# Two attention layers on one core: two heads side by side on row and column tiles, instead of one head over two blocks of keys

## The reference

```python
# layer 0, for each head h (16 heads, 64 columns each)
q, k, v = xn @ Wq[h], xn @ Wk[h], xn @ Wv[h]
attn = softmax(q @ k.T * scale)                 # 2048 x 2048
s += (attn @ v) @ WO[rows of head h]
# layer 1: q and k are rotated (rope), and a distance bias of the head is added
attn = softmax(q @ k.T * scale - p[h] * log1p(a[h] * abs(i - j)))
s += (attn @ v) @ out_w.T[rows of head h]
```

## Time and profile before

| | |
|---|---|
| median of 3 runs | 3421.73 us (3419.06 to 3424.5) |
| the profiled execution's own time | 3421.26 us |
| its span | 3419.4 us |
| TensorE (PE) busy | 3133.3 us (92%) |
| VectorE (DVE) busy | 2356.3 us (69%) |
| ScalarE (ACT) busy | 1427.8 us (42%) |
| GpSimd (POOL) busy | 2394.8 us (70%) |
| DMA, mean over the span | 43 GB/s |

### The profile page before, as it was taken

The page is one execution under the profiler, slowest core; times in us unless marked ns, Lnnn a source line. Parts: engine busy times, 40 slices in busy tenths (PEclk is TensorE's granted clock), DMA queues, the critical chain, the costliest instruction groups (busy, mean ns, idle before and its releaser), DMA issues. The chain is left out here.

```text
span 3419.4 us, 47107 instructions
## 1 busy us (share of the span) xinstructions
PE 3133.3 (92%) x18389; PEld 1247.1 (36%) x18389; DVE 2356.3 (69%) x3610; ACT 1427.8 (42%) x1609; POOL 2394.8 (70%) x1080
## 2 busy tenths in 40 slices
PE   5949999999999999948888985999999999999997
PEld 3414444444444444333333431333333333333333
DVE  6545555555555555351211696999999999999996
ACT  3325555555555555510000222555554555545544
POOL 0019999999999999900000383888888888888887
PEclk9969999999999999958888997999999999999998
DMA  3341111112111111010000133111111111112200
GB/s 80 126 123 26 25 26 26 26 26 49 26 26 26 26 26 25 1 51 0 0 0 0 49 148 97 49 49 49 49 49 49 49 49 49 49 54 60 60 23 13
DMA packets 53617, 148.69 MB, mean 43 GB/s; under 512 B 17155, under 2 KB 24076, under 8 KB 51220
## 3 DMA queue, kind: packets, MB, share of 16 engines
q1 hardware_dynamic: 53396, 145.67, 15.5%
HBM read 110.78 MB, written 34.87 MB: 43 GB/s over the span
## 5 line engine op out<-in xcount | busy, mean ns | idle before, releaser
L847 POOL TENSOR_TENSOR a_total<-a_total,room 128x1024 f32<-128x1024 f32 x768 | 1815.3, 2364 | 141.9 <-ACT room L740 37.3
L650 PE MATMUL a_ov<-room,va 128*64 128x512 f32 x4096 | 991.6, 605 | 0.0
L774 DVE TENSOR_REDUCE a_mx<-a_jb 128x1 f32<-128x1024 f32 x512 | 627.2, 1225 | 508.6 <-PE a_jb L613 508.6
L733 ACT ACTIVATE room<-room,sscale 128x1024 f32<-128x1024 f32 x512 | 588.4, 1149 | 650.5 <-DVE room L794 650.4
L740 ACT ACTIVATE room<-a_st,sscale 128x1024 f32<-128x1024 f32 x512 | 548.8, 1111 | 556.6 <-PE a_st L639 556.6
L769 DVE CUSTOM_DVE_ANT_0 a_junk<-a_jb,a_tab 128x1024 bf16<-128x1024 f32 x512 | 623.8, 1218 | 50.9 <-PE a_jb L613 34.6
L794 DVE TENSOR_TENSOR room<-a_st,a_tab 128x1024 f32<-128x1024 f32 x512 | 623.7, 1219 | 5.2 <-PE a_st L639 3.0
L612 PE MATMUL a_jb<-a_kh,a_qh 64*128 64x512 f16 x1024 | 396.6, 387 | 102.0 <-DMA a_tab<-bias_line 30.9
L847 POOL TENSOR_TENSOR a_total<-room 128x1024 f32<-128x1024 f32 x128 | 302.5, 2363 | 182.4 <-ACT room L733 135.6
L639 PE MATMUL a_st<-a_qh,a_kh 64*128 64x512 f16 x2048 | 394.9, 382 | 21.0 <-DVE room L794 21.0
L650 PEld LDWEIGHTS a_ov<-room,va 128*64 128x64 f32 x4096 | 248.4, 136 | 423.6 <-issue 363.7
(11 more groups left out here) (181 smaller groups left out, 2616.1 us busy)
## 6 DMA issues: line engine op xcount, KB each, us to landing
a_tab<-bias_line SPq DMA_DIRECT2D x16, 1984.0 KB, 12.1
qk_high<-q_oh SPq DMA_DIRECT2D x32, 512.0 KB, 2.6
qk_low<-q_ol SPq DMA_DIRECT2D x32, 512.0 KB, 3.6
a_qh<-qk_high SPq DMA_DIRECT2D x64, 256.0 KB, 4.9
a_kh<-qk_high SPq DMA_DIRECT2D x64, 256.0 KB, 5.7
a_ql<-qk_low SPq DMA_DIRECT2D x64, 256.0 KB, 6.3
a_kl<-qk_low SPq DMA_DIRECT2D x64, 256.0 KB, 6.7
ex_w<-in_L_ffn_W SPq DMA_DIRECT2D x1, 2048.0 KB, 10.5
```

The source lines that it names most:

```text
L650: last = nc.tensor.matmul(ov[t * DH:(t + 1) * DH, :], k.va[:, 2 * s + t, h * DH:(h + 1) * DH], prob[:, step % RING, t * QC:(t + 1) * QC], ...
L733: nc.scalar.activation(prob[:, r, :], prob[:, r, :], ACT.Exp, scale=k.sscale[:, layer:layer + 1])\
L774: nc.vector.reduce_max(mx[:, j // 2, j % 2:j % 2 + 1], jb[:, :], AX.X).then_inc(max_done, 1)
L847: nc.gpsimd.tensor_tensor(t, first, prob[:, step % RING, :], ALU.add).then_inc(summed, 1)
```

## The change

A chunk is now 512 queries of two heads A and B, with one block of 128 keys in a step: 32 chunks (`NCP`) of 16 steps (`NT`). Row half 0 of the array holds head A and row half 1 head B, and the values of A and B land on the two column halves, in the partitions 0 to 63 and 64 to 127 of `ov`. A step has as many matmuls, passes and adds as before. What is different:

- Q and K are loaded once for a pair, and a copy with its halves swapped (`qx`, `kx`) serves the maxima. V is stored to DRAM in `qkv_stage` (`v_store`) and loaded for each pair.
- The softmax sums are made as 64 equal rows for each head (`sums`, step 5), VectorE takes the reciprocal of all 128x512 of them (`invert`), the output is normalised before the projection (`normalise`, VectorE in layer 0, GpSimd in layer 1), one projection of both heads follows at step 9 (`project`), and one VectorE pass adds it to `acc` (`accumulate`).
- GpSimd keeps two running sums, of the even and the odd steps. They are added once a chunk (`fold`): on VectorE in layer 0 at step 2, on GpSimd in layer 1.
- The maxima run 20 steps ahead (`LEAD`), all 20 of them before the first step.

```diff
+NJ = 16
+LEAD = 20
+ADDS = NT - 2
+FOLD_STEP, SUM_STEP, OUT_STEP, MERGE_STEP, ROW_STEP = 2, 5, 9, 11, 13
...
+            for n in range(NV):
+                sp.wait_ge(high, n + 1)
+                sp.wait_ge(low, n + 1)
+                sp.dma_start(k.v_store[:, :, n, :].rearrange("r p d -> p r d"),
+                             vs[:, n % NB, :].rearrange("p (r d) -> p r d", r=H // 2)).then_inc(v_stored[n % NB], 16)
...
+                sp.dma_start(qh[:, at], k.qk_high[0, pr]).then_inc(loaded, 16)
+                sp.dma_start(kh[:, at], k.qk_high[1, pr]).then_inc(loaded, 16)
+                for a in range(2):
+                    here, there = slice(a * DH, (a + 1) * DH), slice((1 - a) * DH, (2 - a) * DH)
+                    sp.dma_start(qx[here, at], k.qk_high[0, pr][there, :]).then_inc(loaded, 16)
+                    sp.dma_start(kx[here, at], k.qk_high[1, pr][there, :]).then_inc(loaded, 16)
...
+                sp.dma_start(va[:, pr % 2, :, :], k.v_store[pr]).then_inc(loaded, 16)
...
-                for t in range(2):
-                    q = (2 * e + t) * P
-                    nc.tensor.matmul(xb[:, 2 * P + t:2 * P + t + 1], total[:, n % 2, q:q + P], k.ones[:, 0:1],
-                                     start=(t == 0), stop=True, skip_group_check=True)
-                for t in range(2):
-                    q = (2 * e + t) * P
-                    last = nc.tensor.matmul(xb[:, t * P:(t + 1) * P], osb[:, q:q + P], k.wo[:, n // NC, :],
-                                            start=False, stop=True, skip_group_check=True)
+                for a in range(2):
+                    last = nc.tensor.matmul(xb[a * DH:(a + 1) * DH, :], k.ones[:, 0:DH], total[:, a * QC:(a + 1) * QC],
+                                            start=True, stop=True)
+                last.then_inc(sum_ready, 1)
+
+            def project(n):
+                pe.wait_ge(normed, n + 1)
+                for q in range(4):
+                    last = nc.tensor.matmul(xb[:, q * P:(q + 1) * P], norm[:, q * P:(q + 1) * P], k.wo[:, n // NC, :],
+                                            start=True, stop=True)
                 last.then_inc(proj_ready, 1)
...
-            def invert(n, e):
-                ve.wait_ge(proj_ready, 2 * n + e + 1)
-                nc.vector.reciprocal(rs[:, e, :], xb[:, 2 * P:2 * P + 2]).then_inc(rs_done, 1)
...
+            def fold(n):
+                ve.wait_ge(summed, ADDS * (n + 1))
+                if n >= 1:
+                    ve.wait_ge(sum_ready, n)
+                nc.vector.tensor_tensor(total[:, :], even[:, :], odd[:, :], ALU.add).then_inc(folded, 1)
+
+            def invert(n):
+                ve.wait_ge(sum_ready, n + 1)
+                if n >= 1:
+                    ve.wait_ge(normed, n)
+                nc.vector.reciprocal(inverse[:, :], xb[:, :]).then_inc(inverted, 1)
+
+            def normalise(n):
+                ve.wait_ge(inverted, n + 1)
+                ve.wait_ge(ov_saved, n + 1)
+                if n >= 1:
+                    ve.wait_ge(proj_ready, n)
+                nc.vector.tensor_tensor(norm[:, :], osb[:, :], inverse[:, :], ALU.mult).then_inc(normed, 1)
+
+            def accumulate(n):
+                ve.wait_ge(proj_ready, n + 1)
+                if n >= NC:
+                    ve.wait_ge(proj_done, n - NC + 1)
+                a = flat(k.acc[:, (n % NC) * 4:(n % NC + 1) * 4, :])
+                nc.vector.tensor_tensor(a, xb[:, :], a, ALU.add).then_inc(proj_done, 1)
...
+                if not bias and s == FOLD_STEP and n >= 1:
+                    fold(n - 1)
+                if s == SUM_STEP and n >= 1:
+                    invert(n - 1)
+                    if not bias:
+                        normalise(n - 1)
+                if s == OUT_STEP and n >= 1:
+                    accumulate(n - 1)
...
+                    nc.gpsimd.tensor_tensor(total_[:, :], first, prob[:, step % RING, :], ALU.add).then_inc(summed, 1)
+                    if bias and s == SUM_STEP + 2 and n >= 1:
+                        normalise(n - 1)
+                if bias:
+                    fold(n)
```

More of the change, by code:

```diff
@@ L579, in attention_stage @@
         block = ctx.enter_context(nc.Block())
         def summed_by(step):
-            n, s = divmod(step, NS)
-            return pool_adds * n + min(max(1, s), pool_adds)
+            n, s = divmod(step, NT)
+            return ADDS * n + (s + 1 if s < 2 else s - 1)
         @block.sync
         def _(sp):
[L587 to L598, removed]
-                if bias:
-                    sp.dma_start(tab[:, h % 2, :], k.bias_rows(h)).then_inc(loaded, 16)
@@ new lines, in project, with ahead, between @@
+            def project(n):
[3 more added lines that the diff above has]
+                                            start=True, stop=True)
+                last.then_inc(proj_ready, 1)
+            def ahead(step):
+                if step + LEAD < NCP * NJ:
+                    maxima(step + LEAD)
+            def between(n, s):
+                if s == SUM_STEP and n >= 1:
+                    sums(n - 1)
+                if s == OUT_STEP and n >= 1:
+                    project(n - 1)
+                if s == ROW_STEP and n + 1 < NCP:
+                    row(n + 1)
@@ L675, in _ @@
             pe.wait_ge(ones_set, 2)
-            for j in range(NJ):
-                maxima(0, j)
+            for job in range(NJ):
+                maxima(job)
             row(0)
-            for j in range(NJ):
-                maxima(1, j)
-            def ahead(n, s):
-                if n + AHEAD < NCH:
-                    maxima(n + AHEAD, s)
-            def between(n, s):
-                if s == ROW_STEP and n + 1 < NCH:
-                    row(n + 1)
-                if s in OUT_STEPS and n >= 1:
-                    project(n - 1, OUT_STEPS.index(s))
@@ L710, in _ @@
-            for s in range(NS - LAG, NS):
-                values(NCH - 1, s)
-            for e in range(2):
-                project(NCH - 1, e)
+            for job in range(NJ, LEAD):
+                maxima(job)
+            if bias:
+                scores(0)
+            for step in range(NCP * NT):
+                n, s = divmod(step, NT)
+                if bias:
+                    if step + 1 < NCP * NT:
+                        scores(step + 1)
+                    ahead(step)
+                    between(n, s)
+                elif s % 2 == 0:
+                    ahead(step)
+                    scores(step)
+                    scores(step + 1)
+                    ahead(step + 1)
+                    between(n, s + 1)
+                if s % 2 == 0 and step >= LAG:
+                    values(step - 2)
+                    values(step - 1)
@@ L715, in _ @@
+            for step in range(NCP * NT - LAG, NCP * NT):
+                values(step)
+            sums(NCP - 1)
+            project(NCP - 1)
         @block.scalar
@@ L829, in _ @@
+            if not bias:
+                fold(NCP - 1)
+            invert(NCP - 1)
+            if not bias:
+                normalise(NCP - 1)
+            accumulate(NCP - 1)
         @block.gpsimd
```

308 lines of the change are left out of this document (155 added, 153 removed).

## The result

The kernel after the change took 3550.64 us (median of 4 runs, 3548.63 to 3553.02) against 3421.84 for the kernel before (median of 4, 3419.06 to 3424.5): ratio 1.0377, 95% interval 1.0359 to 1.0395. Its profiled execution took 3548.63 us with a span of 3546.8, 127.4 more than the span before.

The account below looks back on a forecast made before the run. TensorE was taken to set layer 0's pace, and a loop through TensorE and VectorE layer 1's. Layer 0 +19, layer 1 +62, starts and ends +50 gave 131 us on 3421.26: about 3552, range 3475 to 3620.

Parts of the forecast that it names:

- The reciprocal: VectorE's `invert` of 128x512, priced at 3.4 us from 6.4 ns a column between 2 and 16 columns.
- The rivals with 0.7 and 4.4 us: Reciprocal a plain pass of 0.7 us: total 3379, chance 0.11; dearer than the slope at 4.4 us: 3616, chance 0.08.
- 64 us of time: Cost of each us of reciprocal: 32 + 32 stretches over both layers.
- Layer 0's stall: Step 5: TensorE waits 3.2 us for its second maxima; stretch 38.7 against 38.06 us, +19 us for the layer.
- stretch: 16 steps, two chunks before the change, one after; forecast 38.7 us in layer 0, 42.6 in layer 1.
- Layer 1: Steps 5 and 9: +3.2 us at the maxima, 1.2 for the project pair; 42.6 against 40.68 us, +62 for the layer.
- Starts and ends: Both layers' loads +21, first maxima +13, V stores +8, stage ends +3 and +5: together +50 us, 30 to 85.
- I give the two sums nothing: GpSimd's 14 adds take 33.1 to 34.5 us, under TensorE's 35.4 either way, so two running sums save nothing.
- plain (4.77): Layer 1 pair of steps before the change, 2703.25 to 2708.02, taken as 4.77 us; one with `project` 5.33.

Follow-up runs that it names:

- The copy: Kernel after the change with the 128x512 reciprocal replaced by a plain copy of the same size in both layers: 3354.66 us, ratio 0.9812.
- Kept busy: Kernel after the change, but TensorE computes step 7's scores four times over in layer 0's stall: 3521.69 us, ratio 1.0299.
- chains: Kernel after the change, but GpSimd adds steps 4 to 9 to one sum and 10 to 15 to the other, each add waiting: 3578.9 us, ratio 1.0469.
- multiply from PSUM: Kernel after the change, but layer 0's reciprocal is written back to PSUM and the multiply reads it there: 3491.2 us, ratio 1.0212.
- three pieces: Kernel after the change, reciprocal cut into 171, 171 and 170 columns at steps 5, 7, 9, with later multiply and project: 3400.04 us, ratio 0.9942.
- ScalarE: Kernel after the change, reciprocal made on ScalarE as exp(-ln(x)), layer 0's multiply reading PSUM, multiply and project later: 3331.68 us, ratio 0.9736.

## Why the prediction was right, point by point

3552 was forecast and 3550.64 measured. So close a hit is partly luck: two terms were off by almost 20 us each, in opposite directions.

- **The reciprocal.** 3.4 us from the slope of 2 and 16 columns; measured 3.35. The piece of 171 columns took 1.23, so the slope holds: 6.2 ns a column from 171 to 512. The rivals with 0.7 and 4.4 us are out. The estimate of 4.4 us that I drew from the Trainium skill ("VectorE: DVE Perf Modes") does not hold as I read it.
- **What it costs.** I put each us of it at 64 us of time. The copy took 2.66 us off and saved 193: 73 a us. Without the clock drops (about 17 x 1.65 in layer 0 and 14 x 0.85 in layer 1, 40 us) it is 57 a us.
- **Layer 0's stall.** By the steps of the forecast: invert ends 6.87 us after the pair's first L640 (7.0), the multiply 8.63 (8.75), the second maxima 9.82 (10.15), the next pair starts at 4.99 (5.08); the multiply's wait was 1.04 (1.1), the stall 2.9 (3.2). A short stretch is 38.54 (38.7). The Trainium skill ("GPSIMD Engine Reference", "8. Key points") has GpSimd contend with VectorE's passes of two SBUF inputs; the 1.73 us against 0.69 with one input in PSUM agree.
- **What failed there:** the forecast priced the stall at its length alone and said nothing of TensorE's clock, so it put that cost at nothing. A stall of 2.9 us let it fall to half in 17 of 29 stretches, 1.65 us each. Layer 0's steps cost +38.0 us instead of +19; without the 28 us of it the term would have been +10. Kept busy, TensorE kept its clock and the stretches were 38.55, so the sum of the forecast's own steps was right.
- **Layer 1.** The maxima of step 9 came after 12.53 us (12.75); `project` made its pair some 1.0 us longer (42.25 less 8 x 4.78 and less 2.97; I took 1.2). A short stretch is 42.25, a mean one 42.64 (42.6), since clock drops of 0.85 in half of them fill what I had put too high: luck again. +57.2 instead of +62.
- **Starts and ends.** +50 was too much, +32 measured: loads +10.3 (21), the four maxima +15.4 (16, less 3 that the last steps save, which stand with the steps in the table), V's stores 0 (8), ends +7.6 (8). I took layer 1's extra 4.1 MB at 269 GB/s, 15 us; they took 7.3. That rate was no limit of the loads. A stretch of layer 1's first loads after the change has 402 GB/s:

```profile
2110.00:2115.00 5.00, 0.00 (x0) 0.00 (x0) 0.00 (x0) 0.00 (x0) 0.00 (x0) 0.50 1.02 402
```

- **"I give the two sums nothing"** held for the pace of the adds and failed for the time: with chains the kernel took 31 us more, 25 of them through the multiply's wait and the clock in layer 0. My estimate of the phase allowed 2.33 to 2.46 us from add to add, and did not say that the difference matters.
- **Two readings were off, with little effect.** Four adds in 9.85 us are three pauses and the last add's 2.36, so chained adds start 2.50 us apart and not 2.46; 14 of them are 34.9 us, still under 35.4. The pair of layer 1 that I called plain (4.77) holds `row`; the one without anything is 20.34 - 4.77 - 2 x 5.33 = 4.91. After the change the plain pairs took 4.78, so the sum by 4.77 came out.

## What to carry to other kernels

When a small operation becomes a wide one, price it from the slope of the same operation at other widths, and ask what its engine is late for while it runs: here 3.35 us, 64 times, on the engine that the loop went through, undid a saving of 2.4 and 1.3 us a stretch. Cut it so that a piece fits the slack of a step, or give it to the engine that has room. A stall in which TensorE stands idle can cost more than its length, so look at the granted clock behind it before adding up, and count short waits that stand close together.

## What the runs showed of the hardware

- In layer 0 TensorE's granted clock fell to 0.50 for 3.4 us after a wait of 2.7 us (2.9 by the distance of the maxima) in 17 of 29 stretches, and with chained adds after one of 3.1 in 23 of 29; never after one of 1.7 (1.9 by the same distance, multiply from PSUM), and never when the same time was filled with matmuls. In layer 1 it fell in 14 of 29 stretches behind two waits of 1.62 and 0.75 us, 2.3 us apart, and in none where these waits were gone (copy, three pieces, ScalarE). So the length of the longest wait alone does not tell. What decides between two like stretches stays open.
- A reciprocal took 0.16 us for 2 columns, 0.25 for 16, 1.23 for 171 and 3.35 for 512.
- A VectorE multiply of 128x512 with both inputs in SBUF took 1.73 to 2.1 us (median) beside GpSimd's adds, and 0.69 with one input in PSUM.
- A reciprocal of 128x512 can be written over its input in PSUM in 3.36 us, the same as to SBUF.
- With ln and exp in one set of tables, loaded once a stage, ScalarE's switch between them showed no load: 0.58 and 0.61 us a pass.
- GpSimd's adds of 128x1024 start 2.32 us apart when each is independent of the one before, and 2.50 when it is not.
